# Attention and ternary feed-forward on one core: the product with g moved to VectorE, and the first pass of the loop in another order

## The reference

```python
# attention, 16 heads of 32, 64 features; q from layernorm(x), k and v from ctx
q_prime = relu(q @ Wqf.T); k_prime = relu(k @ Wkf.T) * mask
kv  = einsum('bhnf,bhne->bhfe', k_prime, v)
out = einsum('bhmf,bhfe->bhme', q_prime, kv) / (q_prime . sum(k_prime) + 1e-8)
x   = x + out @ Wo.T + bo
# feed-forward, hidden size 2048; bit_linear rounds its input to 8 bits by row, its weights to -1, 0, 1
gate, up  = bit_linear(layernorm(x), w_gate), bit_linear(layernorm(x), w_up)
activated = up * square(relu(gate))
activated = activated * rsqrt(mean(activated**2) + 1e-6) * g
x = x + bit_linear(activated, w_down)
```

## Time and profile before

| what | value |
|---|---|
| time, median of 3 executions | 458.77 us (457.62, 458.77, 458.94) |
| the profiled execution | 457.62 us, span 455.4 us |
| TensorE busy | 446.0 us, 3315 matmuls |
| VectorE busy | 373.5 us, 656 instructions |
| ScalarE busy | 297.0 us |
| GpSimd busy | 147.6 us |

### The profile page before, as it was taken

One profiled execution on the slowest core, in us unless ns is written; L12 is line 12 of the kernel. 1 busy time (PEld: TensorE's weight loads), 2 busy tenths in 40 slices (PEclk: granted clock), 3 DMA queues, 4 the chain that ended last, 5 costly groups with the idle time before them and its releaser, 6 DMA issues.

```text
span 455.4 us, 8456 instructions
## 1 busy us (share of the span) xinstructions
PE 446.0 (98%) x3315; PEld 353.9 (78%) x3315; DVE 373.5 (82%) x656; ACT 297.0 (65%) x425; POOL 147.6 (32%) x292
## 2 busy tenths in 40 slices
PE   8999999999999999999999999999999999999996
PEld 5899989999999788767786795876777777784443
DVE  4945759549975896999898789998799898888993
ACT  5773978837131447776878678577685877656972
POOL 0000000003530544642441562525465254244450
PEclk9999999999999999999999999999999999999999
DMA  7981464606300300053036025125204221431245
GB/s 252 421 357 47 185 232 150 267 1 241 131 1 1 115 13 14 1 127 59 24 79 108 24 46 129 36 48 94 46 24 81 59 48 32 96 81 21 51 94 162
DMA packets 53081, 45.52 MB, mean 100 GB/s; under 512 B 43441, under 2 KB 44337, under 8 KB 51121
## 3 DMA queue, kind: packets, MB, share of 16 engines
q1 hardware_dynamic: 53040, 44.98, 34.2%
HBM read 27.14 MB, written 4.19 MB: 69 GB/s over the span
## 4 chain that ended last, share of the span: by engine, by line
PE 77%; DVE 11%; DMA 5%; ACT 2%; issue 2%; POOL 1%; SPq 0%; DVEq 0%; ACTq 0%
PE ps L341 72%; PE ps L562 3%; PE ps L593 2%; DVE zb L347 2%; DMA yqTe<-yqb 2%; DMA xs<-in_wu_dram 2%; DMA xs<-in_wk_dram 1%; DVE st L577 1%; ACT yqb L344 1%; DVE kp L350 1%; DMA yqTq<-yqb 1%; DVE tk L769 1%; DVE yqb L796 1%; DVE xs L347 1%; POOL tk L350 1%
## 5 line engine op out<-in xcount | busy, mean ns | idle before, releaser
L341 PE MATMUL ps<-tu,xqT 128*128 128x512 bf16 x256 | 67.7, 386 | 0.2 <-DVE zb L347 0.2
L341 PE MATMUL ps<-tg,xqT 128*128 128x512 bf16 x256 | 67.6, 386 | 0.0
L350 POOL TENSOR_SCALAR tk<-tk 128x1 f32<-128x1 f32 x96 | 36.1, 376 | 46.3 <-DVE tk L720 25.1
L341 PE MATMUL ps<-td,yqT 128*128 128x512 bf16 x208 | 50.7, 385 | 0.0
L344 ACT ACTIVATE qoh<-ps,small 128x256 fp32r<-128x256 f32 x64 | 27.7, 467 | 32.4 <-PE ps L341 32.3
L344 ACT ACTIVATE rb<-zb 128x1024 f32<-128x1024 f32 x29 | 30.7, 1060 | 22.6 <-DVE zb L347 22.6
L344 ACT ACTIVATE rb<-ps 128x1024 f32<-128x1024 f32 x29 | 29.6, 1020 | 22.9 <-PE ps L341 21.9
L347 POOL TENSOR_TENSOR zb<-zb,g_b 128x1024 f32<-128x1024 f32 x12 | 28.7, 2388 | 43.4 <-ACT rb L344 30.7
L347 DVE TENSOR_TENSOR zb<-ps,rb 128x1024 f32<-128x1024 f32 x29 | 35.3, 1218 | 8.6 <-PE ps L341 6.1
L341 PEld LDWEIGHTS ps<-tu,xqT 128*128 128x128 bf16 x256 | 25.1, 99 | 22.0 <-DVE zb L347 0.9
L341 PE MATMUL ps<-kvh,apl 128*128 128x66 f32 x112 | 41.6, 371 | 0.0
(11 more groups left out here) (154 smaller groups left out, 1348.5 us busy)
## 6 DMA issues: line engine op xcount, KB each, us to landing
xs<-in_wg_dram SPq DMA_DIRECT2D x4, 1024.0 KB, 13.0
xs<-in_wu_dram SPq DMA_DIRECT2D x4, 1024.0 KB, 5.5
xs<-in_wd_dram SPq DMA_DIRECT2D x4, 1024.0 KB, 8.9
xs<-in_x_dram SPq DMA_DIRECT2D x8, 512.0 KB, 4.2
out_dram<-xs SPq DMA_DIRECT2D x15, 256.0 KB, 2.1
craw<-in_ctx_dram SPq DMA_DIRECT2D x7, 512.0 KB, 7.6
qoh<-qol SPq DMA_DIRECT2D x12, 128.0 KB, 2.3
qy<-qol SPq DMA_DIRECT2D x12, 128.0 KB, 2.3
```

The lines of the kernel that those rows point to most:

```text
L341: return add("pe", name, cost, waits, lambda e: e.matmul(out, lhsT, rhs, start=start, stop=stop))
L350: return add(lane, name, cost, waits, lambda e: e.tensor_scalar(out, a, s1, s2, op0, op1))
```

## The change

Twelve more of the 32 Y run on VectorE, so that all do. Six fewer yk do (1, 7, 16, 25, 27 and 28 go to ScalarE, 30 stays). Six more yb run on VectorE (1, 4, 5, 7, 20 and 23), four stay on ScalarE. In the loop the text of the first gate and up is written the same way for all p; for p = 0 it now stands between quads 0 and 1 and quads 2 and 3 of s3, where before it followed s3 and was part of the interleaved list. MIXED was (1, 2, 3, 4), which the new condition gives too.

```diff
-Y_ON_DVE = (1, 3, 4, 6, 7, 8, 11, 13, 14, 15, 19, 21, 22, 23, 25, 26, 27, 28, 30, 31)
-YK_ON_DVE = (1, 7, 16, 25, 27, 28, 30)
-YB_ON_ACT = (1, 4, 5, 7, 20, 23, 27, 28, 29, 31)
+Y_ON_DVE = tuple(range(32))
+YK_ON_DVE = (30,)
+YB_ON_ACT = (27, 28, 29, 31)
-MIXED = (1, 2, 3, 4)
@@
         for p in range(NB - 2):
             a, n = p + 1, p + 2
-            first = gate_up(2 * p, 0)
-            if p:
-                mix(first, [])
-                first = []
-            s3(a)
+            early = (0, 1) if p == 0 else ()
+            s3(a, early)
+            mix(gate_up(2 * p, 0), [])
+            s3(a, [q for q in range(4) if q not in early])
             if p:
                 kv_blocks(a)
             side = s4(a, 0) + s4(a, 1)
             side.insert(36, lambda: s5(a, 0))
-            main = first + gate_up(2 * p, 1) + (down(2 * p - 1) if p in MIXED else []) + gate_up(2 * p + 1, 0) + gate_up(2 * p + 1, 1)
+            main = gate_up(2 * p, 1) + (down(2 * p - 1) if 0 < p < NB - 3 else []) + gate_up(2 * p + 1, 0) + gate_up(2 * p + 1, 1)
```

## The result

| what | before | after |
|---|---|---|
| median of 5 executions | 458.77 us | 461.81 us |
| range | 457.62 to 459.95 | 460.80 to 463.53 |
| ratio, with its 95% interval | | 1.0076 (1.0048 to 1.0102) |
| the profiled execution | 457.62 us, span 455.4 | 461.57 us, span 459.8 |
| Y on GpSimd / VectorE | 12 / 20 | 0 / 32 |

The changed kernel is 0.76% slower, about 3.0 us; the prediction had 1.3. A second set of its executions beside three other kernels gave 1.0086 (1.0058 to 1.0115).

What follows compares the result with a forecast made beforehand. TensorE, busy 446.0 of 455.4 us, was taken as the bound, with VectorE and ScalarE setting the last 30 us. Terms +0.6 - 0.5 + 1.2 = +1.3, laid on the median 458.77, gave 460.1 us; range 457.8 to 462.5.

Steps and rivals of the forecast that it cites:

- Part a: TensorE's order in pass p = 0: denser interleaving +1.1 us, a removed wait -0.47, together +0.6.
- The wait before quad 2: TensorE in s3(1) of pass 0: the 0.31 us wait, 0.47 counted start to start, goes as G0.0 and U0.0 fill it.
- Part b: VectorE's load in the passes: net +8.2 us of work there, effect on the time -0.5 us, between -1.4 and +0.8.
- the walk through p = 1 to 4: Following p = 1 step by step: inputs come 0.4 us or more before TensorE's use, so passes 1 to 4 cost nothing.
- The rival in which VectorE becomes the bound: Passes p = 0 to 4 each give TensorE a 0.5 to 1 us wait: +4.3 us, 463.1; chance 0.15.
- new waits at `qf6.3` and `on13.1`: Pass 5: ym20 ahead of qf6.3's rows and ym21 ahead of on13.1, each good for up to 0.4 us.
- Nothing new: Pass 5: no new TensorE waits; with all three old waits gone as well, the case was priced at -1.4 us.
- Part c: The end, from 409 us, following VectorE and ScalarE: +1.2 us, between +0.8 and +1.6.
- ScalarE at the end: Two extra activations between 428.92 and 435.02 us make yb29 end 1.6 us later.
- the landing: Last transposes: tile 14's second half takes 3.09 to 4.73 us, tile 15's first 3.09; the end moves +1.2.
- The freed GpSimd: Rival: VectorE is never stopped, Y come 1.2 us sooner, end waits shrink: -2.7 us, 456.1; chance 0.12.
- The terms: Rival for the whole sum: gains in the passes offset a 0.8 us loss at the end: 458.8 to 459.3; chance 0.25.

Runs made afterwards that it cites:

- y_only: The kernel before, old loop order, with all 32 Y on VectorE and yk and yb unchanged: 461.70 us, ratio 1.0057 to before.
- best_try: The kernel before, old loop: Y except 24, 29 and yk 25, 27, 28, 30 on VectorE, yb as changed, ym22, yb20 after am12: 460.24 us, 1.0018.
- mid_fix12: Changed kernel with Y24, Y29 on GpSimd, yk25, 27, 28 on VectorE, and ym22, yb20 held behind am12: 458.96 us, ratio 0.9988 to before.
- sets_mid: Changed kernel with Y24 and Y29 back on GpSimd and yk25, 27 and 28 back on VectorE: 460.02 us, ratio 1.0019 to before.
- yk_back: Changed kernel with yk25, yk27 and yk28 back on VectorE, Y24 and Y29 still there: 460.19 us, ratio 1.0024 to before.
- yk27_28: Changed kernel with yk27 and yk28 back on VectorE, yk25 left on ScalarE: 460.63 us, 460.13 at full clock, ratio 1.0043 to before.
- loop_only: Changed loop order with the Y, yk and yb sets of the kernel before: 460.21 us, ratio 1.0016 to before.
- after_again: The changed kernel run once more, nothing altered, beside other kernels: 461.76 us, ratio 1.0086 to before.
- outs_after: Changed kernel with the output DMAs of tiles 12 and 13 held until tile 15's second transpose has landed: 462.22 us, one execution.
- fix12: Changed kernel with ym22 and yb20 held on VectorE until am12 is done: 462.02 us, ratio 1.0053 to before; 460.26 in one full-clock execution.

## Why the prediction was right and wrong

The time, 461.81, lies in the range (457.8 to 462.5), and the direction of the forecast was right. But the sum was 1.7 us too small (2.0 in the traces, from the common point), and mostly for a reason that it didn't have. That the miss in the time is not larger is in part luck: the 0.4 us between span and time that the moved Y give back were in no term. Its steps in turn:

- **Part a, right, and a little high.** +0.33 against +0.6. The wait before quad 2 went, and the dense stretch cost about what p = 5 had shown. What the step lacked is the coupling: it priced the order as if the Y stayed where they were. y_only and best_try show that in the old order pass 0 costs 1.3 us or more with the same Y.
- **Part b, VectorE's load in the passes: the walk through p = 1 to 4 held, nearly.** From the queries of sequence 2 to those of sequence 6, passes 1 to 4, 0.2 us came in where nothing was priced. 37.85 us for pass 1 before and after, and VectorE at 34.59 of them where 36.1 was worked out. The rival in which VectorE becomes the bound did not come. No `yb` took over 1.4 us any more, where one had 2.87. The wait at the queries of sequence 7 shrank by 0.5, as worked out, but it didn't arrive in the sum: at those queries the kernel stands at +0.43, after +0.33 behind pass 0. The 0.2 of passes 1 to 4 and new losses in pass 5, the wait of 0.26 us for `apl` among them, took it back.
- **Part b, the step that failed: what was moved ahead of what in pass 5.** The text named ym20 and ym21 and looked for new waits at `qf6.3` and `on13.1`. The price was paid by ym22, yb20 and the order on SP, and the one who waited was G12.0, for xqT12: +1.3 us. "Nothing new" had been the middle value. That transpose had 3.3 us of slack in the trace of before, and for that reason I hadn't followed it. Such a slack is used up by a few instructions of 0.7 to 1.6 us and a transpose that goes first on SP. mid_fix12 against sets_mid shows its size: 1.1 to 1.4 us, returned by two waits on VectorE.
- **Part c, ScalarE at the end: right.** yb29 +1.4 (predicted +1.6), ym31 and yb30 +0.9 (predicted +1.05). yk_back and yk27_28 show that yk27 and yk28 on ScalarE cost 1.5 us of the time at full clock (461.6 against 460.1), but the traces put only 0.5 to 0.6 of it behind the common point, and most of that in the landing.
- **Part c, the landing: mis-sized, and for the wrong one.** The prediction took 4.73 us for tile 14's second half as a possible value and 3.09 for tile 15 as given. It was 3.10 for the first and 4.25 for the second, and only the second was on the path. That is +1.8 instead of +1.2, 0.2 over the upper end. The reading behind the term was off too: not half, but three of the four halves in the trace of before took about 3.1 (3.05, 3.09 and 3.09). And loop_only, with the sets of before, also lost 0.8 us at the end, so not all of the +1.8 belongs to the change.
- **The rivals.** The freed GpSimd did not pay: ScalarE's row decided, as said. The terms did not cancel.

## What to carry to other kernels

When work moves onto an engine with a fixed order, list every product of that engine that someone waits for, also those with some us of slack, and recount their slack with the new order; here the loss came at the one with 3.3 us. Price edits together where one gives the time that the other spends. And before a trace is used as the base of a sum, compare its execution with the median: ours was the fastest of its kernel, and its luck sat in just the waits that the sum was made of.

## What the runs showed of the hardware

**TensorE's clock after the last wait.** An execution's mean granted clock was 1.000 or about 0.996, and those at 0.996 are longer: 459.9 against 459.0 for the kernel before (18 of 76 executions), 462.1 against 460.1 for yk27_28 (5 of 11), and 463.4 against 461.6 for the changed kernel (7 of 14; two of them, at 461.62 and 461.81, are as quick as one at full clock). The trace shows where it is. Windows of after, then of after_again, 450 to 455 and 455 to 460 (columns as above, PEclk third from the right):

```profile
450.00:455.00 5.00, 2.27 (x19) 1.60 (x18) 0.75 (x1) 0.00 (x0) 0.00 (x0) 1.00 0.98 161
455.00:460.00 5.00, 1.94 (x18) 1.48 (x16) 0.97 (x2) 0.00 (x0) 0.00 (x0) 1.00 0.15 52
```

```profile
450.00:455.00 5.00, 3.31 (x18) 2.48 (x19) 0.24 (x1) 0.00 (x0) 0.00 (x0) 0.72 0.53 131
455.00:460.00 5.00, 2.02 (x16) 1.44 (x13) 0.97 (x2) 0.00 (x0) 0.00 (x0) 0.84 0.15 52
```

And the last link of the chain in each, D15's 32 matmuls:

```profile
453.27 3.68 PE ps L340 x32
```

```profile
451.69 5.35 PE ps L340 x32
```

TensorE had waited 2.7 us before D15 in after and 2.2 in after_again. There the granted clock was 1.00 up to 452, 0.60 in the next us and 0.50, that is 1.2 GHz, in the two after it, and 1.00 again from 456 on; the same matmuls then took 5.35 us and not 3.68, 1.7 more. The two kernels with 0.6 us of wait before D15 (mid_fix12, best_try) had it in none of 24 executions, but sets_mid with 1.8 in none of 11, yk_back with 1.7 in 1 of 12, and the kernel before, whose trace has 0.44, in 18 of 76, so the wait alone doesn't decide. The Trainium skill's page TensorE: Matmul & The Clock Gate (Part 1: The HAM clock gate) says that the lower clock is the default and that activity of the array releases the full one; the traces agree in so far as the fall came during this wait (outs_after) or 0.5 to 1.3 us after it (after_again, fix12).

**Two executions part before the loop.** The start of the loop varied by 1.7 us between the 14 traces, in the same code. In that of after the whole shift against before arose in the first 25 us, beside the first loads. For differences of 1 to 3 us shifts have to be counted from a common point behind it.

**GpSimd and VectorE.** With the Y gone from GpSimd, `kvl` still took 1.56 us where 0.42 was the rule: it started at 376.08, and an `xbo` had run on GpSimd from 376.06 to 377.35. In before the same `kvl` started at 375.28, 0.03 us ahead of its `xbo`, and took 0.40. The SBUF page of the Trainium skill (SBUF — State Buffer, section "SBUF: two separate sides") calls the ports that the two engines share an exclusive lock, which whoever starts first holds for the whole instruction. The traces agree with that for short instructions as well: what is left on GpSimd can still stop one on VectorE. Here it cost nothing that a run shows, since fix12 has the same 1.56 and no wait for xqT12.
